# A graph network's score stage: who makes the one-hots of a block's last rows

## The reference

```python
f1 = relu(x[row] @ nb_W[l] + nb_b[l])
f2 = relu(x[col] @ self_W[l] + self_b[l])
h = relu(concatenate([f1, f2], axis=1) @ att1_W[l] + att1_b[l])
log_alpha = (h @ att2_W[l] + att2_b[l])[:, 0]
mask = clip(sigmoid(log_alpha) * (ZETA - GAMMA) + GAMMA, 0.0, 1.0)
rowsum = segment_sum(mask, row) + 1e-06
d_inv_sqrt = clip(rowsum ** (-0.5), 0.0, 10.0)
vals = mask * d_inv_sqrt[row] * d_inv_sqrt[col]
x = segment_sum(vals[:, None] * x[col], row)
```

## Time and profile before

| | |
|---|---|
| median of 3 runs | 10621.58 us (10617.47 to 10626.42) |
| the profiled execution | 10631.04 us |
| its span in the trace | 10629.3 us, mean granted TensorE clock 0.917 |
| the first layer's score stage | about 1600 to 3456 us of the span |
| PE, DVE busy over the span | 79%, 78% |
| ACT, POOL busy over the span | 26%, 43% |

### The profile page before, as it was taken

How to read it: one execution, slowest core, us unless ns; L and a number is a source line. 1 busy time by engine, 2 the same in 40 slices (tenths; PEclk the granted TensorE clock), 3 DMA queues, 4 the chain that set the end, 5 groups by cost and what they waited for, 6 DMA issues and landing times. The chain is left out here.

```text
span 10629.3 us, 718909 instructions
## 1 busy us (share of the span) xinstructions
PE 8424.6 (79%) x288474; PEld 7559.1 (71%) x288474; DVE 8245.8 (78%) x13852; ACT 2745.6 (26%) x5816; POOL 4528.4 (43%) x4893
## 2 busy tenths in 40 slices
PE   0011028888888899979999899979999899969996
PEld 0010017777777788869999788869999788858885
DVE  8997148888888777767777777767777777787775
ACT  0010014444444333310000333310000333323332
POOL 0001731111111788821111788821111688858883
PEclk9855569999999999989999999989999999989997
DMA  1000017777676555547777555547777555545552
GB/s 26 0 0 11 19 48 223 223 220 221 218 221 209 148 161 160 162 130 212 213 212 210 149 161 160 161 129 211 212 214 212 147 160 160 160 116 162 160 161 72
DMA packets 1006492, 1635.93 MB, mean 154 GB/s; under 512 B 260770, under 2 KB 745352, under 8 KB 1005960
## 3 DMA queue, kind: packets, MB, share of 16 engines
q1 hardware_dynamic: 952134, 1581.31, 50.2%
q0 software_dynamic: 54272, 53.46, 2.4%
HBM read 1348.02 MB, written 286.27 MB: 154 GB/s over the span
## 5 line engine op out<-in xcount | busy, mean ns | idle before, releaser
L907 PE MATMUL bank<-tab,extra 128*64 128x64 bf16 x201684 | 3986.0, 197 | 432.6 <-DVEq L1380 180.7
L907 PEld LDWEIGHTS bank<-tab,extra 128*64 128x64 fp8e4 x201684 | 3564.5, 112 | 922.0 <-issue 862.7
L685 POOL TENSOR_TENSOR planes<-planes 128x448 f32<-128x448 f32 (+1 forms) x2744 | 2610.5, 963 | 552.1 <-DVE planes L1543 494.5
L617 POOL DMA_INDIRECT xg<-q_table,ixb x588 | 647.2, 1101 | 3675.2 <-ACT ixb L757 3430.4
L1005 PE MATMUL bank<-planes,extra 128*128 128x192 bf16 x19992 | 2099.7, 247 | 41.8 <-POOL planes L685 11.6
L793 ACT CAST bank<-planes 128x448 f32<-128x448 bf16 (+1 forms) x2744 | 1515.3, 552 | 2347.3 <-DVE planes L1536 2338.7
L1536 DVE TENSOR_TENSOR planes<-bank,mask_all 128x448 f32<-128x448 f32 (+2 forms) x2744 | 1704.2, 621 | 215.4 <-PE bank L907 134.6
L1543 DVE TENSOR_TENSOR planes<-planes,bank 128x448 f32<-128x448 f32 (+1 forms) x2744 | 1733.2, 632 | 126.9 <-ACT bank L793 126.9
L1415 DVE SCALAR_TENSOR_TENSOR extra<-bank,a2w 128x448 f32<-128x448 f32 (+1 forms) x2058 | 1300.3, 640 | 587.5 <-PE bank L930 526.1
L1005 PEld LDWEIGHTS bank<-planes,extra 128*128 128x128 fp8e4 x19992 | 1586.8, 96 | 173.4 <-issue 38.2
L930 PE MATMUL bank<-plb,extra 128*128 128x64 bf16 x44982 | 1610.2, 195 | 4.7 <-issue 4.7
(11 more groups left out here) (213 smaller groups left out, 4374.6 us busy)
## 6 DMA issues: line engine op xcount, KB each, us to landing
extra<-one_hots SPq DMA_DIRECT2D x1372, 368.0 KB, 3.3
extra<-one_hots SPq DMA_DIRECT2D x2156, 224.0 KB, 3.7
extra<-one_hots SPq DMA_DIRECT2D x588, 192.0 KB, 2.4
one_hots<-extra SPq DMA_DIRECT2D x490, 224.0 KB, 2.3
one_hots<-extra SPq DMA_DIRECT2D x294, 368.0 KB, 2.9
work<-slot_rows_cols SPq DMA_DIRECT2D x196, 368.0 KB, 4.3
work<-slot_rows_cols SPq DMA_DIRECT2D x294, 224.0 KB, 3.9
work<-slot_rows_cols SPq DMA_DIRECT2D x98, 192.0 KB
```

Of the source, the lines that this page charges most:

```text
L617: nc.gpsimd.indirect_dma_start(out=to, out_offset=None, in_=table_d, in_offset=bass.IndirectOffsetOnAxis(ap=index, axis=0)).then_inc(done, 16)
L685: nc.gpsimd.tensor_tensor(tiles(yrl[:, 2, a * C:b * C]), tiles(yrl[:, 1, a * C:b * C]), upper[:, 1, a:b, :], ALU.subtract).then_inc(low_re ...
L907: mm = pe.matmul(bank[half * S:(half + 1) * S, i * C:(i + 1) * C], oct_[:, k * P + half * S:k * P + (half + 1) * S], tab[:, at:at + C], st ...
```

## The change

DVE's `make` of ort2 at the head of each block goes. ACT makes this piece instead, by two activations of 128x1792: `Abs` of the row number minus the partition's number (bias `minus_p`, a new constant that POOL writes once), stored as bf16 in a free part of `work` (`apart`), and `Relu` of one minus that, stored in fp8. It stands in ACT's queue behind the sigmoid of the block before and ahead of the 15 copies of turned tiles. The piece gets a semaphore of its own, `last_made`, and `made` counts five a block.

```diff
                     for kind in KINDS:
-                        wait_alone(sp, made, value(sp, R * len(KINDS) + MADE[kind]))
+                        if kind == LAST_MADE:
+                            wait_alone(sp, last_made, value(sp, R + 1))
+                        else:
+                            wait_alone(sp, made, value(sp, R * NV + MADE[kind]))
                         store(R, piece(kind), made_out[kind])
...
+            nc.gpsimd.iota(minus_p[:], [[1, 1]], base=0, channel_multiplier=-1, allow_small_or_imprecise_dtypes=True)
...
+                def last_one_hots(R, late):
+
+                    lo, hi = piece(LAST_MADE)
+                    if late:
+                        wait_alone(act, last_made, value(act, R))
+                    wait_alone(act, rb_in[LAST_MADE], value(act, R * 16 + 16))
+                    nc.scalar.activation(apart, rb[:, lo:hi], ACT.Abs, bias=minus_p[:, 0:1]).then_inc(apart_ready, 1)
+                    if late:
+                        wait_alone(act, turn_one_hots, value(act, R * NT))
+                        wait_alone(act, made_out[LAST_MADE], value(act, R * 16))
+                    wait_alone(act, apart_ready, value(act, R + 1))
+                    nc.scalar.activation(oh1[:, lo:hi], apart, ACT.Relu, bias=1.0, scale=-1.0,
+                                         saturate=False).then_inc(last_made, 1)
...
                     if late:
                         sigmoid(value(act, n - 1))
                     if first:
+                        last_one_hots(R, late)
                         turned_one_hots(t)
...
-                        if first:
-                            wait_alone(pe, made, n * len(KINDS) + MADE["ort", FIRST_OF[g]])
+                        if first and ("ort", FIRST_OF[g]) == LAST_MADE:
+                            wait_alone(pe, last_made, n + 1)
+                        elif first:
+                            wait_alone(pe, made, n * NV + MADE["ort", FIRST_OF[g]])
...
-                    make(("ort", 2), R, (turn_one_hots, value(dve, R * NT)) if late else None)
                     if late:
                         masks(value(dve, R - 1), value(dve, R - 1))
```

More of the change, by code:

```diff
@@ L82, in gnn_kernel @@
     KINDS = list(MADE)
+    LAST_MADE = KINDS[-1]
+    NV = len(KINDS) - 1
     ROUNDS = -(-(E // S + NB) // XP)
@@ L103, in gnn_kernel @@
         iota_pi = sb("iota_pi", [P, 1], I32)
+        minus_p = sb("minus_p", [P, 1])
         iota_k = sb("iota_k", [P, XP])
@@ L172, in gnn_kernel @@
         rb = work[:].bitcast(U8)[:, 0:TS + MS]
+        apart_at = (TS + MS) // 4 + 512
+        apart = work[:].bitcast(BF16)[:, 2 * apart_at:2 * apart_at + (CUTS[PIECES[2][1]] - CUTS[PIECES[2][0]]) * P]
         yv_at = OHW // 4
@@ L260, in gnn_kernel @@
         made = sem("one_hots_made")
+        apart_ready = sem("distances_ready")
+        last_made = sem("last_one_hots_made")
         made_out = {k: sem(f"made_out_{k[0]}{k[1]}") for k in KINDS}
@@ L895, in cols @@
                     if first:
-                        wait_alone(pe, made, t * len(KINDS) + MADE["oct", FIRST_OF[g]])
+                        wait_alone(pe, made, t * NV + MADE["oct", FIRST_OF[g]])
                     else:
```

## The result

The changed kernel takes 10570.9 us (median of 5 runs, 10565.2 to 10576.2) against 10621.6: a ratio of 0.9951, 95% interval 0.9936 to 0.9965, so 0.5% or 51 us faster, interval 37 to 68 us. Its profiled execution took 10565.2 us, the one of before 10631.0; both lie off their medians, in opposite directions, so the two traces differ by 66 us where the medians differ by 51.

What follows compares the result with a forecast made beforehand. DVE was taken to lead each score-stage block at both ends, PE between. 43 us from the block heads plus 10 us from the clock gave a 53 us gain: 10621.6 to 10569 us, range 10532 to 10618.

Steps and rivals of the forecast that it cites:

- What bounds the block: First layer's score stage: DVE leads each 18.34 us block at both ends, PE between; PE idles 0.85 us for `sums`.
- The cover: Block head on DVE: the make covers a 0.54 us sigmoid wait, so 0.44 us gained a block, 43 us in all.
- ACT: ACT's pair takes 3.6 us in a 4.86 us hole before the first copy, 1.0 us to spare, costing nothing.
- SP's queue: SP's stores of ort2 and oct0 go out later, oct0's at most 0.8 us after its piece is made; cost nothing.
- The gaps on PE: PE's idle time shrinks about 0.3 us before the row sums and 0.15 us before the second `turn`.
- The clock's term: Score stage: a fifth fewer of 41 long blocks, in which PE's clock falls to 1.2 GHz; 10 us gain.
- A: Rival: PE's gaps close so far that nearly no block is long, about 10528 us; chance 0.12.
- B: Rival: half as many long blocks again from PE's clock, gain only 15 us, 10607 us; chance 0.07.
- C: Rival: Abs needs another ACT table, two loads a block, 81 us slower, 10703 us; chance 0.06.
- D: Rival: ACT's pair takes double, 7.1 us, making the third `turn` late; 132 us slower; chance 0.03.
- E: Rival: PE's part starts no earlier, something else of PE or ACT comes last; within 20 us; chance 0.06.

Runs made afterwards that it cites:

- sums_first: The changed kernel with DVE making oct0 behind `sums` instead of ahead of the second `hidden`: 10482.5 us, ratio to before 0.9867.
- one_more_abs: The changed kernel with one more Abs of 1792 columns on ACT ahead of the pair: 10560.5 us, ratio to before 0.9943.
- delay_tail: The changed kernel with an addition of 128x344 on DVE between the last make and last `hidden` of each block: 10607.1 us, ratio to before 0.9981.
- after_again: The changed kernel run again unaltered, on a chip of the slower kind: 11552.1 us against 11444.3 for before there, ratio 1.0096.
- two_more_abs_b: The changed kernel with two more Abs, 1792 and 1664 columns, on ACT ahead of the pair, first kind of chip: 10779.8 us, ratio to before 1.0133.

## Why the prediction was right, point by point

- **What bounds the block** held: DVE at both ends, PE between, and PE's part starts when `sums` does. The head's gain came out at the end of every quick block, 18.34 - 17.90 = 0.44 us, and sums_first shows the same link from the other side: with `sums` earlier, the block is shorter by another 0.59 us.
- **The cover** held to the hundredth: 0.54 us of wait, forecast from the second layer's, so 0.44 us gained of the 1.07 that the make took. A forecast by busy time, 97 x 1.15 = 111 us, would have been off by a factor of two.
- **ACT** held: 1.77 + 1.70 + 0.1 us of pauses against 3.6, 0.95 us of idle time against 1.0. The Trainium skill's rule (page "ScalarE: Activation LUTs", section "Rules for kernel authors") sends relu-like work to VectorE, up to about three times faster per element in bf16. The trace agrees that VectorE is faster, but one activation against one comparison is 1.77 to 1.14 us, a factor of 1.5; the prediction's factor of three compares a pair with a single instruction. Speed doesn't decide here anyway: one_more_abs puts half as much again on ACT for nothing. The Trainium skill's section "Table sets: the hidden batching unit" on the same page has abs in every set, and the trace agrees: no load for Abs.
- **SP's queue** held in its effect, nobody waits, and was a little off in its size. Its timeline in the changed kernel, 2317.7 to 2319.6 us, answers to the earlier trace rows:

```profile
2317.76 0.33 SPq L465 DMA_DIRECT2D one_hots<-extra  x1
...
2318.27 0.35 SPq L460 DMA_DIRECT2D work<-slot_rows_cols  x1
...
2319.22 0.33 SPq L465 DMA_DIRECT2D one_hots<-extra  x1
```

  The store of ort2 goes out 4.1 us behind `logits` instead of 1.3, and that of oct0 5.6 us behind instead of 4.9, 1.4 us after its piece is made (2316.09 + 1.75) where 0.8 were forecast. The forecast gave each issue 0.5 us; from the numbers to the next store SP took 0.95 us.
- **The gaps on PE** were placed wrong. Forecast was 0.3 us less before the row sums and 0.15 less before the second `turn`. It was all before the row sums, which start 0.44 us earlier (2.66 to 2.22 us from the end of `logits`), and 0.02 before the `turn`. The step took the modelled end of the matmuls before as a bound, but the row sums (2315.88) started 0.13 us before that modelled end.
- **The clock's term** had the right sign and was too small: 10 us, a fifth of the long blocks; measured 16 us by delay_tail (19 less the 3 of its shorter quick block) and 29 us between the two traces, 41 to 23. The sum of the terms by the experiments, 43 + 16 = 59, lies within the interval of the gain (37 to 68) and above its middle. Its sign had a reason, the gaps on PE; its size was a guess from no row.
- **Rivals.** A and B (nearly no long blocks; half as many again) didn't come, but A's state exists, in sums_first. C (tables) and D (slow activations) fell. E's sense, that something else leads the head of the block, is what happens on the other kind of chip, where the sign is the other one too. No rival had that: the forecast holds for chips that behave like the one of the rows.

## What to carry to other kernels

The worth of work taken off the leading engine is its length less the wait that it stood over; look for a place in the same trace where that wait stands bare (here the second layer), and it is priced exactly. Where idle time on PE falls can count as well as how long it is: here 0.3 us more close behind matmuls of few columns brought the clock down in 18 more blocks, and as much delay in a dense stretch in none. And a gain of half a percent at the head of a loop body may change its sign on another chip; run both kernels on more than one before keeping it.

## What the runs showed of the hardware

- The twelve experiments ran on four chips of two kinds: before took 10626 and 10637 us on two of them (10622 at the prediction) and 11398 and 11444 us on the other two, with the same program. Each chip was used at one time only, so whether this belongs to the chip or to its state then isn't shown. Outside the first layer's score stage the traces take 8790 to 8803 us on the first kind and 9545 to 9604 on the second. Part of it are pauses of PE, most of about 0.5 us, in the midst of matmuls that wait for nothing. Behind the stage, in after (3400 to 10500 us) and in after_again (3600 to 11500 us), total us, times and longest:

```profile
PE bank L933 <- issue: 56.5, 202, 1.8
...
PE bank L933 <- issue: 543.9, 1159, 2.1
```

- With the same work and the same length of block, 1.1 instead of 0.8 us of idle time close behind 51 matmuls of 4 columns gave 38 instead of 20 of 95 blocks in which the granted clock falls from 2.4 to 1.2 GHz. With no wait for `sums` there, in sums_first, whose block is a microsecond shorter too, it was none; with a second wait of 1.24 us behind the 0.83, in two_more_abs_b, it was all. A fall costs a block 1.0 to 1.3 us here, and 2.2 us in the longest ones of before (20.5 us).
- An activation of 128x1792 from 8-bit integers to bf16 took 1.77 us, from bf16 to fp8 1.70. The rows of f32 activations with a bias gave 1.75 us for this width, an estimate.
